# An attention and mixture-of-experts block on one core: expert gates turned on VectorE and fetched back for the biases, and the last batch decoded twice, the second time with weights scaled by ln_g and centred

## Chip, cores and metric

The kernel runs on one core of one Trainium2 chip. The metric is the device time of one execution in microseconds (us), the median of several runs. All arithmetic is float32, but for some bfloat16 copies of bias rows.

## What is computed

Four batches of 512 tokens with 128 channels go through attention and then through a feed-forward part with eight experts, each part with a layer norm before and after and a residual around it:

```python
x = x + ln(attn(ln(x)))                      # one head of 128; ln without weights
x = x + ln(ffn(ln(x)))
# ffn, per token:
spikes = sigmoid(h @ W_enc + b_enc)          # 128 -> 256
cont   = spikes @ W_s2c + b_s2c              # 256 -> 64
probs  = softmax(cont @ Wr + br)             # 8 experts
gate   = top-2 of probs, normalised, 0 for the other six
y      = sum_e gate[e] * (relu(cont @ W1[e] + b1[e]) @ W2[e] + b2[e])
spikes = sigmoid(y @ W_c2s + b_c2s)          # 64 -> 256
decoded = spikes @ W_dec + b_dec             # 256 -> 128
return (decoded - mean) * rsqrt(var + eps) * ln_g + ln_b
```

So the end of a batch has two layer norms in a row: the one of the ffn with `ln_g` and `ln_b` (LN_DEC in the code), and the outer one without weights (LN_Z).

## The kernel before

The program is written engine by engine; each engine runs its list in order and waits on semaphores (`d_` of a DMA, `pe_` of TensorE, `a_` of ScalarE, `v_` of VectorE, `g_` of GpSimd). In the profile TensorE is PE, its weight load PEld, VectorE DVE, ScalarE ACT, GpSimd POOL and SyncE SP. A float32 matmul shows as two MATMUL records. Tokens are in T = 4 tiles of 128; "halves" are tiles 0, 1 and 2, 3. Tiles with a dimension of 2 after the partitions alternate between even and odd batches. The eight PSUM banks are `ps_s` (2), `ps_t`, `ps_a`, `ps_o` (2) and `ps_c` (2).

The batches overlap: while the attention of batch m = b + 2 runs, the experts of batch b are computed, in the loop `for b in range(2)` of each engine's list; after it comes a straight list for the rest of batches 2 and 3.

The gates of a batch take this way. `route` (PE) multiplies into the logits, 8 per token. `router_top`, `router_index` and `router_gates` (DVE, L1175 to L1215) find the two largest and write `gate`, with a token per partition. `turn_gates` (PE, L850) turns the four tiles, so that an expert is a partition. `gate_out` (ACT) copies them to `gateT` (L535), and its DMA (L537, on ACT's queue) writes them to DRAM, eight rows of 2 KB. When that has landed, SP issues five fetches (L379) that broadcast the rows to all 128 partitions of `gate_all`: experts 0, 1, 2 and 3, 4 and 5, 6 and 7, 256 KB an expert. `gate_hidden(b, e)` (DVE, L1224) multiplies the hidden values of expert e in PSUM (from `hidden_pair`, PE, L881) by its gates and writes `gated`, which `expert_out` (PE, L905) takes. `expert_biases` (PE, L899) multiplies `gateT` by `b2_plus` into the same bank first.

The mean over channels of `decoded` is taken out ahead of time: `w_dec` and the bias are centred over the channels, so `decoded` in PSUM has mean zero. Of the last batch, `decode_part` (PE, L934) makes it in halves, `dec_square` (ACT, L561) sums its squares, `dec_var` (DVE, L1245) adds eps, and `inverse_std` (POOL, L406) takes the power -0.5. `dec_scale` (DVE, L1237) multiplies by `ln_g`, `z_scale` (L1254) by the inverse deviation and adds `ln_b`; `z_stats` (L1115 to L1120) takes mean and variance of z, POOL the power again, ACT subtracts the mean (`z_centre`, L574), and `z_add` (L1278) makes the output of that half, which `store` (SP, L371) writes. `x_stats` and `x_norm` (L1127) are the norm at the start of a batch; `turn_x` (PE, L725) waits for it.

## Time and profile before

| | us |
|---|---|
| median of 3 runs (131.42 to 131.71) | 131.65 |
| the profiled execution's own time | 131.94 |
| its span, first to last instruction | 130.1 |
| busy in the span: PE, DVE, ACT, POOL | 118.0, 92.6, 61.3, 30.5 |

The span is what the profile shows; its time is 1.8 us more. Times in rows count from the span's start. "Idle before" in brackets is how long the engine sat idle just before, with what ended it. The profile is of one execution, whose own time is 0.29 us above the median.

### The profile page before, as it was taken

How to read it: one execution, taken by the hardware profiler on the slowest of the kernel's cores; microseconds unless marked ns; L12 is line 12 of the kernel's file. 1: busy time of each engine (PE TensorE's matmuls, PEld its weight loads, DVE VectorE, ACT ScalarE, POOL GpSimd, SP SyncE). 2: the span in 40 equal slices, each digit the busy share in tenths (PEclk: the TensorE clock that was granted, in tenths of full speed). 3: DMA queues.
4: the chain of work that ended last, by engine and by line, in shares of the span. 5: the costliest groups of instructions: out<-in, count | busy, mean ns of one | idle time of the engine just before them, and what ended most of it. 6: DMA issues, size and time to landing. Idle time of an engine off the chain costs nothing.

```text
span 130.1 us, 2478 instructions
## 1 busy us (share of the span) xinstructions
PE 118.0 (91%) x813; PEld 79.4 (61%) x813; DVE 92.6 (71%) x392; ACT 61.3 (47%) x177; POOL 30.5 (23%) x61
## 2 busy tenths in 40 slices
PE   6899999999998999999999998999999999998400
PEld 2556686878645887663677983657566556665300
DVE  0858537698989755888246178968949996689792
...
PEclk9999999999999999999999999999999999999955
...
DMA packets 8843, 12.37 MB, mean 95 GB/s; under 512 B 2641, under 2 KB 5470, under 8 KB 8830
## 3 DMA queue, kind: packets, MB, share of 16 engines
...
q8 instruction: 6, 0.10, 0.3%
...
## 4 chain that ended last, share of the span: by engine, by line
PE 58%; DVE 19%; DMA 8%; POOL 4%; ACT 4%; issue 3%; POOLq 1%; SPq 1%; DVEq 0%
PE ps_t L905 9%; PE ps_s L760 7%; PE ps_o L785 6%; PE ps_s L881 5%; DMA gate_all<-gates 5%; PE ps_o L814 4%; POOL rstd L406 4%; PE ps_t L772 3%; DVE stats L1115 3%; PE ps_c L881 3%; PE ps_c L917 2%; PE ps_a L829 2%; DMA x_in<-in_L_attn_x 2%; DVE gated L1224 2%; ACT probs L495 2%
## 5 line engine op out<-in xcount | busy, mean ns | idle before, releaser
L406 POOL TENSOR_TENSOR rstd<-var_eps,minus_half 128x2 f32<-128x2 f32 (+1 forms) x33 | 25.4, 771 | 93.7 <-DVE var_eps L1120 45.8
L785 PEld LDWEIGHTS ps_o<-v,probsT 128*128 128x128 f32 x128 | 15.7, 191 | 3.5 <-ACT probsT L500 2.5
L785 PE MATMUL ps_o<-v,probsT 128*128 128x128 f32 x128 | 17.5, 279 | 0.1
L905 PE MATMUL ps_t<-gated,w 128*64 128x256 f32 x128 | 16.8, 389 | 0.6 <-DVE gated L1224 0.5
L495 ACT ACTIVATE probs<-ps_s,neg_max 128x512 f32<-128x512 f32 x16 | 11.0, 687 | 11.0 <-DVE neg_max L1143 10.4
L760 PE MATMUL ps_s<-xnT,yT 128*128 128x512 f32 x32 | 16.0, 596 | 0.1
L1143 DVE TENSOR_REDUCE neg_max<-ps_s 128x1 f32<-128x512 f32 x16 | 10.9, 689 | 6.0 <-PE ps_s L760 5.9
L905 PEld LDWEIGHTS ps_t<-gated,w 128*64 128x64 f32 x128 | 8.0, 136 | 8.4 <-DVE gated L1224 4.1
L1224 DVE SCALAR_TENSOR_TENSOR gated<-ps_s,b_minus,gate_all 128x512 f32<-128x512 f32 x14 | 9.9, 745 | 3.3 <-PE ps_s L881 1.8
L516 ACT ACTIVATE spikes<-ps_o,bias_half 128x512 f32<-128x512 f32 x6 | 4.1, 688 | 15.1 <-PE ps_o L814 15.1
L500 ACT ACTIVATE probsT<-ps_t 128x512 f32<-128x512 f32 x16 | 9.5, 592 | 2.0 <-PE ps_t L772 1.8
L772 PE MATMUL ps_t<-ident,probs 128*128 128x128 f32 x64 | 9.8, 276 | 0.2 <-ACT probs L495 0.2
L772 PEld LDWEIGHTS ps_t<-ident,probs 128*128 128x128 f32 x64 | 7.3, 141 | 4.2 <-ACT probs L495 2.4
L1224 DVE SCALAR_TENSOR_TENSOR gated<-ps_c,b_minus,gate_all 128x512 f32<-128x512 f32 x12 | 8.4, 745 | 1.0 <-PE ps_c L881 0.5
L881 PE MATMUL ps_s<-cont,w 64*128 64x256 f32 x56 | 7.9, 401 | 0.0
L541 ACT ACTIVATE moeT<-ps_t 128x256 f32<-128x256 f32 x4 | 1.5, 384 | 12.1 <-PE ps_t L905 12.1
L760 PEld LDWEIGHTS ps_s<-xnT,yT 128*128 128x128 f32 x32 | 5.2, 191 | 2.8 <-issue 2.4
L1155 DVE SCALAR_TENSOR_TENSOR var_eps<-square_sum,eps_term 128x2 f32<-128x2 f32 x8 | 1.3, 164 | 7.4 <-ACT squares L506 7.3
L881 PE MATMUL ps_c<-cont,w 64*128 64x256 f32 x48 | 6.3, 380 | 0.0
L1162 DVE SCALAR_TENSOR_TENSOR x_mid<-ps_o,rstd,x_in 128x128 f32<-128x128 f32 x16 | 4.8, 343 | 2.0 <-POOL rstd L406 2.0
L881 PEld LDWEIGHTS ps_s<-cont,w 64*128 64x128 f32 x56 | 4.8, 186 | 2.1 <-issue 1.5
L1118 DVE BATCH_NORM_AGGREGATE mean_var<-stats 128x2 f32<-128x6 f32 x48 | 6.0, 165 | 0.0
...
## 6 DMA issues: line engine op xcount, KB each, us to landing
gate_all<-gates SPq DMA_DIRECT2D x12, 512.0 KB, 6.2
...
x_in<-in_L_attn_x SPq DMA_DIRECT2D x2, 128.0 KB, 2.7
out<-x_out SPq DMA_DIRECT2D x2, 128.0 KB, 1.8
w_enc<-in_L_ffn_W_enc SPq DMA_DIRECT2D x1, 128.0 KB, 2.8
```

The costliest lines, as they stand in the source:

```text
L406: nc.gpsimd.tensor_tensor(rstd[part], var_eps[part], minus_half[:, t0:t1], ALU.pow).then_inc(g_rstd[n], 1)
L495: nc.scalar.activation(probs[:, b % 2, t], ps_s[:, t % 2], ACT.Exp, bias=neg_max[:, b % 2, t:t + 1], accum_out=prob_sum[:, b % 2, t:t + 1] ...
L500: nc.scalar.activation(probsT[:, b % 2, t], ps_t[:, :].rearrange("p (k q) -> p k q", k=T), ACT.Identity).then_inc(a_pT, 1)
L760: nc.tensor.matmul(ps_s[:, t % 2], yT[:, b % 2, t * P:(t + 1) * P], xnT[:, b % 2], start=True, stop=True).then_inc(pe_s, 1)
L772: mm = nc.tensor.transpose(ps_t[:, k * P:(k + 1) * P], probs[:, b % 2, t, k * P:(k + 1) * P], ident[:, :])
L785: mm = nc.tensor.matmul(attn_out(t), probsT[:, b % 2, t, k], v[:, b % 2, k], start=(k == 0), stop=(k == T - 1))
L814: nc.tensor.matmul(enc_bank(b, c), w_enc[:, c * P:(c + 1) * P], hT[:, b % 2], start=True, stop=True).then_inc(pe_enc, 1)
L881: mm = nc.tensor.matmul(hidden_banks(b, e)[:, h], w1[half, e], cont[half, b % 2], start=True, stop=True)
L905: mm = nc.tensor.matmul(ps_t[h * M:(h + 1) * M, 0:SH], w2[:, e], gated[:, e, h * SH:(h + 1) * SH], start=False, stop=(e == E - 1))
L1118: nc.vector.bn_aggr(mean_var[:, n, b % 2, t], stats[:, n, b % 2, t]).then_inc(v_mv[n], 1)
L1143: nc.vector.tensor_reduce(neg_max[:, b % 2, t:t + 1], ps_s[:, t % 2], AX_X, ALU.max, negate=True).then_inc(v_max, 1)
L1224: nc.vector.scalar_tensor_tensor(token_halves(gated[:, e]), hidden_banks(b, e), b1_minus[:, e:e + 1], token_halves(gate_all[:, b % 2, e]), ...
```

## The change

It has three parts.

*Gates.* `turn_gates` and the copy to `gateT` by ACT are gone for all four batches. DVE writes `gate` with the expert ahead of the tile and turns it in blocks of 32 by 32 into `gate_blocks`, 128 partitions by 32. The DMA on ACT's queue takes that to the same place in DRAM, now as 128 pieces of 128 bytes. SP fetches the eight rows back into `gateT` for `expert_biases`, ahead of the five fetches of `gate_all`.

*Order around the logits of batch 2.* `to_cont(2)` is put between experts 5 and 6 of batch 1, `route(2)` and `hidden_pair(2, 0)` ahead of `to_spikes(1)`. On ACT `cont_out(2)` and `second_exp(2)` go forward, and `cont_out(3)` ahead of `dec_square(1, 0)`. On DVE `z_stats(0, 0)` goes behind the router of batch 2.

*Last batch.* POOL makes `w_dec * ln_g` and `bias * ln_g`, DVE centres these and `ln_b` over the channels (`scaled_weights`), and POOL splits the bias into three bfloat16 rows. After `decode_part` PE decodes both halves again with them. z is then read from PSUM, times the inverse deviation, plus the centred `ln_b`, and has mean zero: `dec_scale`, `z_means` and the subtraction on ACT go away for this batch. The variance of the first half comes from a sum of squares on ACT, of the second from DVE's statistics as before.

```diff
@@ -375,6 +396,10 @@
                 sp.wait_ge(d_gate_out[b], 16)
                 if b >= 2:
                     sp.wait_ge(v_gated, E * (b - 1))
+                    sp.wait_ge(pe_moe, b - 1)
+                else:
+                    sp.wait_ge(g_zero_rows, 4)
+                sp.dma_start(gateT[0:E, b % 2], gates_dram[b].ap()).then_inc(d_gateT[b % 2], 16)
                 for j, (e0, e1) in enumerate(FETCHES):
                     sp.dma_start(gate_all[:, b % 2, e0:e1],
                                  gates_dram[b].ap()[e0:e1].partition_broadcast(P)).then_inc(d_gate_in[b % 2][j], 16)
...
             inverse_std(LN_X, 3, 0)
+            pool.wait_ge(v_wdec, 8)
+            pool.wait_ge(v_bdec, 1)
+            pool.wait_ge(d_ln, 32)
+            nc.gpsimd.tensor_tensor(w_scaled[:, :, :], w_dec[:, :, :],
+                                    g_all[:, :].unsqueeze(1).to_broadcast([P, HC, D]), ALU.mult).then_inc(g_scaled, 1)
+            nc.gpsimd.tensor_tensor(b_scaled[:, :], b_dec_sum[:, :], g_all[:, :], ALU.mult).then_inc(g_scaled, 1)
...
+
+            pool.wait_ge(v_scaled, 2 * (HC + 2) + HC + 2)
+            nc.gpsimd.tensor_copy(b_z_hi[:, :], b_z[:, :]).then_inc(g_bz, 1)
+            pool.wait_ge(g_bz, 1)
+            nc.gpsimd.tensor_tensor(b_z_rest[:, :], b_z[:, :], b_z_hi[:, :], ALU.subtract).then_inc(g_bz, 1)
+            pool.wait_ge(g_bz, 2)
...
             def gate_out(b):
-                act.wait_ge(pe_gT, b + 1)
-                if b == 0:
-                    act.wait_ge(g_zero_rows, 4)
-                if b >= 2:
-                    act.wait_ge(d_gate_out[b - 2], 16)
-                nc.scalar.activation(gateT[0:E, b % 2], gates_bank(b)[0:E], ACT.Identity).then_inc(a_gT, 1)
-                act.wait_ge(a_gT, b + 1)
-                act.dma_start(gates_dram[b].ap(), gateT[0:E, b % 2]).then_inc(d_gate_out[b], 16)
+                act.wait_ge(v_gate_blocks, b + 1)
+                act.dma_start(gates_dram[b].ap().rearrange("e (t j r) -> j (e t) r", t=T, r=32),
+                              gate_blocks[:, b % 2]).then_inc(d_gate_out[b], 16)
...
-            def z_centre(h):
-                act.wait_ge(v_mean, h + 2)
-                for t in range(*HALVES[h]):
-                    nc.scalar.activation(zn[:, (B - 1) % 2, t], z[:, (B - 1) % 2, t], ACT.Identity,
-                                         bias=minus_mean[:, (B - 1) % 2, t:t + 1]).then_inc(a_zn, 1)
+            def z_square():
+                act.wait_ge(v_z, T * (B - 1) + TH)
+                for t in range(TH):
+                    nc.scalar.activation(z_squares[:, t], z[:, (B - 1) % 2, t], ACT.Square,
+                                         accum_out=z_square_sum[:, t:t + 1]).then_inc(a_z_square, 1)
...
@@ -656,16 +698,19 @@
                     exps(m + 1, 1)
                 else:
                     hT_out(3)
-                moe_out(b)
-                cont_out(n)
+                if more:
+                    moe_out(b)
+                    cont_out(n)
+            cont_out(2)
+            moe_out(1)
+            second_exp(2)
             for c in range(HC):
                 spike2(1, c)
-            second_exp(2)
             spike(3, 0)
             spike(3, 1)
             gate_out(2)
+            cont_out(3)
             dec_square(1, 0)
-            cont_out(3)
             dec_square(1, 1)
...
-            def turn_gates(b):
-                pe.wait_ge(v_gate, 9 * (b + 1))
-                if b == 1 or b == 2:
-                    pe.wait_ge(a_c2s, HC * b)
-                for t in range(T):
-                    mm = nc.tensor.transpose(gates_bank(b)[0:E, t * P:(t + 1) * P], gate[:, b % 2, t], ident[:, :])
-                mm.then_inc(pe_gT, 1)
-
...
                 if b < 2:
                     if p == 1:
-                        pe.wait_ge(a_gT, b + 1)
+                        pe.wait_ge(v_logit, b + 1)
+                        pe.wait_ge(a_c2s, HC * b)
...
@@ -884,7 +921,7 @@
 
 
             def expert_biases(b):
-                pe.wait_ge(a_gT, b + 1)
+                pe.wait_ge(d_gateT[b % 2], 16 * (b // 2 + 1))
...
+
+            def decode_scaled(h):
+                b = B - 1
+                t0, t1 = HALVES[h]
+                if h == 0:
+                    pe.wait_ge(g_bz, 7)
+                    pe.wait_ge(v_z1, parts_done(LN_DEC, b - 1, 0))
+                bank = scaled_bank(h)
+                nc.tensor.matmul(bank[:, t0 * P:t1 * P].rearrange("p (t d) -> p t d", d=D), ones_bf[:, :],
+                                 b_z_stack[:, :].unsqueeze(1).to_broadcast([P, t1 - t0, D]), start=True, stop=False)
+                for t in range(t0, t1):
+                    for c in range(HC):
+                        mm = nc.tensor.matmul(bank[:, t * P:(t + 1) * P], spikes2[:, b % 2, c, t * P:(t + 1) * P],
+                                              w_z[:, c], start=False, stop=(c == HC - 1 and t == t1 - 1))
+                mm.then_inc(pe_scaled, 1)
...
-                for e in range(4, E):
-                    expert_out(b, e)
-                to_cont(n)
-                to_spikes(b)
-                route(n)
+                if more:
+                    for e in range(4, E):
+                        expert_out(b, e)
+                    to_cont(n)
+                    to_spikes(b)
+                    route(n)
+            expert_out(1, 4)
+            expert_out(1, 5)
+            to_cont(2)
+            expert_out(1, 6)
+            expert_out(1, 7)
+            route(2)
             hidden_pair(2, 0)
+            to_spikes(1)
             encode(3, 0)
             encode(3, 1)
-            turn_gates(2)
...
@@ -1212,7 +1269,12 @@
                 dve.wait_ge(v_gate, count + 5)
                 nc.vector.tensor_tensor(pick2[:, i], pick2[:, i], wide(w_second), ALU.mult).then_inc(v_gate, 1)
                 dve.wait_ge(v_gate, count + 7)
-                nc.vector.tensor_tensor(gate[:, i], pick1[:, i], pick2[:, i], ALU.add).then_inc(v_gate, 2)
+                nc.vector.tensor_tensor(gate[:, i].rearrange("p e t -> p t e"), pick1[:, i], pick2[:, i],
+                                        ALU.add).then_inc(v_gate, 2)
+                dve.wait_ge(v_gate, count + 9)
+                if b >= 2:
+                    dve.wait_ge(d_gate_out[b - 2], 16)
+                nc.vector.transpose(gate_blocks[:, i], gate[:, i].rearrange("p e t -> p (e t)")).then_inc(v_gate_blocks, 1)
...
+            def scaled_weights():
+                dve.wait_ge(g_scaled, 2)
+                sources = [w_scaled[:, c] for c in range(HC)] + [b_scaled[:, :], b_all[:, :]]
+                results = [w_z[:, c] for c in range(HC)] + [b_z[:, :], b_centred[:, :]]
+                for k, source in enumerate(sources):
+                    nc.vector.bn_stats(scaled_stats[:, k], source).then_inc(v_scaled, 1)
+                dve.wait_ge(v_scaled, HC + 2)
+                for k in range(HC + 2):
+                    nc.vector.bn_aggr(scaled_mean[:, k], scaled_stats[:, k]).then_inc(v_scaled, 1)
+                dve.wait_ge(v_scaled, 2 * (HC + 2))
+                for k, (source, result) in enumerate(zip(sources, results)):
+                    nc.vector.tensor_scalar(result, source, scaled_mean[:, k, 0:1], None, ALU.subtract).then_inc(v_scaled, 1)
+
+            def z_last(h):
+                b = B - 1
+                dve.wait_ge(g_rstd[LN_DEC], parts_done(LN_DEC, b, h))
+                dve.wait_ge(pe_scaled, h + 1)
+                dve.wait_ge(v_scaled, 3 * (HC + 2))
+                for t in range(*HALVES[h]):
+                    nc.vector.scalar_tensor_tensor(z[:, b % 2, t], scaled_bank(h)[:, t * P:(t + 1) * P], inv(LN_DEC, b, t),
+                                                   b_centred[:, :], ALU.mult, ALU.add).then_inc(v_z, 1)
+
+            def z_last_var():
+                dve.wait_ge(a_z_square, TH)
+                nc.vector.tensor_scalar(var_eps[:, LN_Z, (B - 1) % 2, 0:TH], z_square_sum[:, :], 1.0 / D, EPS,
+                                        ALU.mult, ALU.add).then_inc(v_veps[LN_Z], 1)
...
             row_max(3, 0)
             row_max(3, 1)
+            scaled_weights()
             router_top(1)
...
             dec_var(0, 0)
             z_scale(0, 0)
-            z_stats(0, 0)
             router_top(2)
             router_index(2)
             router_gates(2)
+            z_stats(0, 0)
...
             z_add(2, 0)
             dec_var(B - 1, 0)
-            dec_scale(B - 1, 0)
             dec_var(B - 1, 1)
-            z_scale(B - 1, 0)
-            z_stats(B - 1, 0)
-            z_means(B - 1, 0)
-            dec_scale(B - 1, 1)
-            z_scale(B - 1, 1)
+            z_last(0)
+            z_last(1)
+            z_last_var()
             z_stats(B - 1, 1)
-            z_means(B - 1, 1)
             z_add(B - 1, 0)
             z_add(B - 1, 1)
```

Three places of the order. First ACT, from `cont_out(2)` to the gates of batch 3. Here `cont` is written by `cont_out`, `moeT` by `moe_out`, `e` by `second_exp`, `spikes<-ps_c` by `spike2` and `spikes<-ps_o` by `spike`. Before:

```order
L523 ACTIVATE cont<-ps_a,b_cont 128x256
L545 ACTIVATE spikes<-ps_c,bias_half 128x512 x2
L527 ACTIVATE e<-top_diff 128x4
L516 ACTIVATE spikes<-ps_o,bias_half 128x512 x2
L535 ACTIVATE gateT<-ps_c 8x512
L537 DMA gates<-gateT 8x512
L561 ACTIVATE dec_squares,dec_square_sum<-ps_t 128x128 x2
L523 ACTIVATE cont<-ps_a,b_cont 128x256
L561 ACTIVATE dec_squares,dec_square_sum<-ps_c 128x128 x2
L527 ACTIVATE e<-top_diff 128x4
L535 ACTIVATE gateT<-ps_a 8x512
L537 DMA gates<-gateT 8x512
```

Now:

```order
L569 ACTIVATE cont<-ps_a,b_cont 128x256
L583 ACTIVATE moeT<-ps_t 128x256
L573 ACTIVATE e<-top_diff 128x4
L587 ACTIVATE spikes<-ps_c,bias_half 128x512 x2
L562 ACTIVATE spikes<-ps_o,bias_half 128x512 x2
L578 DMA gates<-gate_blocks 4x32x32
L569 ACTIVATE cont<-ps_a,b_cont 128x256
L603 ACTIVATE dec_squares,dec_square_sum<-ps_t 128x128 x2
L603 ACTIVATE dec_squares,dec_square_sum<-ps_c 128x128 x2
L573 ACTIVATE e<-top_diff 128x4
L578 DMA gates<-gate_blocks 4x32x32
```

The copy to `gateT` is gone, and the DMA of batch 2's gates still stands behind both `spikes<-ps_o` of batch 3.

Then PE in the same place: `ps_t<-gated` is `expert_out(1, ...)`, `ps_a<-spikes` is `to_cont`, `ps_c<-moeT` is `to_spikes(1)`, `ps_o<-w_r` is `route(2)`. Before:

```order
L905 MATMUL ps_t<-gated,w 64x256 x8
L829 MATMUL ps_a<-spikes,w_s2c 64x256 x4
L917 MATMUL ps_c<-moeT,w_c2s 128x256 x4
L841 MATMUL ps_o<-w_r,cont 128x8 x4
L881 MATMUL ps_s<-cont,w 128x256 x4
L814 MATMUL ps_o<-hT,w_enc 128x512 x2
L850 MATMUL ps_c<-ident,gate 8x128 x4
L923 MATMUL ps_t<-b_dec_stack,ones_bf 128x256
L950 MATMUL ps_t<-w_dec,spikes 128x128 x4
```

Now:

```order
L942 MATMUL ps_t<-gated,w 64x256 x4
L873 MATMUL ps_a<-spikes,w_s2c 64x256 x4
L942 MATMUL ps_t<-gated,w 64x256 x4
L885 MATMUL ps_o<-w_r,cont 128x8 x4
L918 MATMUL ps_s<-cont,w 128x256 x4
L954 MATMUL ps_c<-moeT,w_c2s 128x256 x4
L858 MATMUL ps_o<-hT,w_enc 128x512 x2
L960 MATMUL ps_t<-b_dec_stack,ones_bf 128x256
L1002 MATMUL ps_t<-w_dec,spikes 128x128 x4
```

The logits of batch 2 come ahead of `to_spikes(1)`; the turn of the gates (`ps_c<-ident,gate`) is gone.

Last DVE at the end of the program, from the first z of the last batch (`dec_var` of both halves stands ahead of it in both, with one `dec_scale` between before). Before:

```order
L1254 SCALAR_TENSOR_TENSOR z<-z,rstd,b_all 128x128 x2
L1115 BN_STATS stats<-z 128x6 x2
L1118 BN_AGGR mean_var<-stats 128x2 x2
L1120 TENSOR_SCALAR var_eps<-mean_var 128x2
L1263 TENSOR_SCALAR minus_mean<-mean_var 128x2
L1237 TENSOR_TENSOR z<-ps_o,g_all 128x256
L1254 SCALAR_TENSOR_TENSOR z<-z,rstd,b_all 128x128 x2
L1115 BN_STATS stats<-z 128x6 x2
L1118 BN_AGGR mean_var<-stats 128x2 x2
L1120 TENSOR_SCALAR var_eps<-mean_var 128x2
L1263 TENSOR_SCALAR minus_mean<-mean_var 128x2
L1278 SCALAR_TENSOR_TENSOR x_out<-zn,rstd,x_mid 128x128 x4
```

Now:

```order
L1343 SCALAR_TENSOR_TENSOR z<-ps_a,rstd,b_centred 128x128 x2
L1343 SCALAR_TENSOR_TENSOR z<-ps_o,rstd,b_centred 128x128 x2
L1348 TENSOR_SCALAR var_eps<-z_square_sum 128x2
L1172 BN_STATS stats<-z 128x6 x2
L1175 BN_AGGR mean_var<-stats 128x2 x2
L1177 TENSOR_SCALAR var_eps<-mean_var 128x2
L1366 SCALAR_TENSOR_TENSOR x_out<-z,rstd,x_mid 128x128 x4
```

With `dec_var` and the first `dec_scale`, the last batch's 20 instructions ahead of its outputs become 12.

## Rows read from the trace of the kernel before

**Rows 1.** The page, parts 1 and 2: busy time, and 40 slices of the span

```profile
PE 118.0 (91%) x813; PEld 79.4 (61%) x813; DVE 92.6 (71%) x392; ACT 61.3 (47%) x177; POOL 30.5 (23%) x61
...
PEclk9999999999999999999999999999999999999955
```

**Rows 2.** Chain of waits, 60 to 82 us: start, us, what

```profile
70.28 0.45 PE ps_c L850 x4
...
71.37 1.45 DMA gates<-gateT
...
73.67 5.95 DMA gate_all<-gates
...
79.72 0.76 DVE gated L1224
```

**Rows 3.** Timeline, 36 to 60 us: start, us, engine line op out<-in xcount

```profile
44.62 1.01 POOL L406 TENSOR_TENSOR rstd<-var_eps,minus_half 128x4 f32<-128x4 f32 x1 [5.55 <-DVE var_eps L1120]
...
46.09 1.10 DVE L1127 TENSOR_SCALAR xn<-x_in,mean_var,rstd 128x128 f32<-128x128 f32 x4
```

**Rows 4.** Timeline, 0 to 36 us

```profile
12.57 0.54 POOL L426 TENSOR_SCALAR w_s2c<-w_s2c_raw 128x128 f32<-128x128 f32 x1
12.62 0.60 DVE L1127 TENSOR_SCALAR xn<-x_in,mean_var,rstd 128x128 f32<-128x128 f32 x2 [0.33 <-POOL rstd L406]
```

**Rows 5.** Timeline, 60 to 82 us

```profile
66.16 0.19 DVE L1175 TENSOR_TENSOR logits<-ps_o,br_all 128x32 f32<-128x32 f32 x1 [3.47 <-PE ps_o L841]
...
69.92 0.60 ACT L500 ACTIVATE probsT<-ps_t 128x512 f32<-128x512 f32 x1
...
70.11 0.60 PE L850 MATMUL ps_c<-ident,gate 128*8 128x128 f32 x4
...
70.56 1.16 PE L785 MATMUL ps_o<-v,probsT 128*128 128x128 f32 x8
...
80.52 1.31 PE L905 MATMUL ps_t<-gated,w 128*64 128x256 f32 x8 [0.55 <-DVE gated L1224]
```

**Rows 6.** Timeline, 82 to 105 us

```profile
93.18 0.69 ACT L516 ACTIVATE spikes<-ps_o,bias_half 128x512 f32<-128x512 f32 x1 [0.17 <-PE ps_o L814]
...
94.36 0.27 ACTq L537 DMA_DIRECT2D gates<-gateT  x1
...
100.01 1.41 DVE L1224 SCALAR_TENSOR_TENSOR gated<-ps_s,b_minus,gate_all 128x512 f32<-128x512 f32 x2
...
101.47 1.41 DVE L1224 SCALAR_TENSOR_TENSOR gated<-ps_c,b_minus,gate_all 128x512 f32<-128x512 f32 x2
```

**Rows 7.** Timeline of SP's queue, 95 to 98 us

```profile
95.82 2.22 SPq L379 DMA_DIRECT2D gate_all<-gates  x5
```

**Rows 8.** DMA issues of 96.6 to 97.05 us: size, us to landing

```profile
gate_all<-gates SPq DMA_DIRECT2D x1, 512.0 KB, 4.7
```

**Rows 9.** DMA issues of the whole span: size, us to landing

```profile
out<-x_out SPq DMA_DIRECT2D x2, 128.0 KB, 1.8
...
b_qk<-in_L_attn_bk ACTq DMA_DIRECT2D x1, 0.5 KB, 3.1
```

**Rows 10.** Timeline, 120.6 us to the end

```profile
120.66 1.06 PE L934 MATMUL ps_o<-w_dec,spikes 128*128 128x128 f32 x8
...
120.86 1.14 DVE L1278 SCALAR_TENSOR_TENSOR x_out<-zn,rstd,x_mid 128x128 f32<-128x128 f32 x4 [0.34 <-POOL rstd L406]
...
122.16 1.36 POOL L406 TENSOR_TENSOR rstd<-var_eps,minus_half 128x2 f32<-128x2 f32 x2 [1.33 <-DVE var_eps L1245]
...
122.89 0.61 DVE L1254 SCALAR_TENSOR_TENSOR z<-z,rstd,b_all 128x128 f32<-128x128 f32 x2 [0.30 <-POOL rstd L406]
123.53 0.49 DVE L1115 BATCH_NORM_STATS2 stats<-z 128x6 f32<-128x128 f32 x2
...
126.57 0.80 POOL L406 TENSOR_TENSOR rstd<-var_eps,minus_half 128x2 f32<-128x2 f32 x1 [1.35 <-DVE var_eps L1120]
...
127.40 0.61 DVE L1278 SCALAR_TENSOR_TENSOR x_out<-zn,rstd,x_mid 128x128 f32<-128x128 f32 x2 [0.26 <-POOL rstd L406]
```

More of the change, by code:

```diff
@@ L229, in c2s_done, with scaled_bank @@
             return b + 1 + (c if b == B - 1 else 0)
+        def scaled_bank(h):
+            return ps_o[:, 1] if h else ps_a
         d_x = [[sem(f"d_x{b}{i}") for i in range(1 if b else 2)] for b in range(B)]
@@ L243, in attention_moe_block @@
         d_ln = sem("d_ln")
+        d_gateT = [sem(f"d_gateT{i}") for i in range(2)]
         d_gate_out = [sem(f"d_gate_out{b}") for b in range(B)]
@@ L257, in attention_moe_block @@
         g_out = sem("g_out")
+        g_scaled = sem("g_scaled")
+        g_bz = sem("g_bz")
         pe_wqk = sem("pe_wqk")
@@ L682, in _ @@
                 dec_square(B - 1, h)
-            for h in range(2):
-                z_centre(h)
+            z_square()
         @block.tensor
@@ L1031, in _ @@
                     turn_h(n)
-                if more:
-                    turn_gates(b)
                 scores(m, 3)
-                if not more:
-                    turn_gates(b)
                 attend(m, 1)
@@ L1107, in _, with statistics @@
                 decode_part(3, h)
+            for h in range(2):
+                decode_scaled(h)
         @block.vector
         def _(dve):
-            def statistics(n, b, i, source):
+            def statistics(n, b, i, source, elsewhere=0):
                 t0, t1 = parts(n, b)[i]
```

46 lines of the change are left out of this document (33 added, 13 removed).

## The prediction

> **What bounds the kernel now.** I read the page first: PE is busy 118.0 of 130.1 us at full clock until the last two slices, where the granted clock is 0.5 (1.2 in place of 2.4 GHz) and PE has no work left [rows 1]. So what shortens the kernel is PE work taken out where PE is not waiting for something else, and the tail behind PE's last matmul. Then the chain of waits shows where that is so. Around the gates of batch 1 it leaves PE: the turn of the gates ends at 70.73, the write to DRAM goes out at 71.37 and lands 1.45 later, and the third fetch of `gate_all` lands at 79.62, just before `gate_hidden(1, 2)` at 79.72 [rows 2]. The timeline shows PE idle 0.55 behind it [rows 5]. In batch 2 the fetch of experts 2 and 3, the first of 512 KB, is issued at about 96.7 and takes 4.7 [rows 7, 8]: it lands at about 101.4, and its reader starts at 101.47 [rows 6]. The fetches are thus nearly the limit in both. In the tail, from PE's last matmul (ends 121.72) to the last output (127.40 + 0.61 = 128.01), one chain goes DVE, POOL, DVE, POOL, DVE [rows 10].
>
> I count against the profiled execution: 131.94 us, 0.29 above the median of 131.65. A difference of 0.2% is about what a measurement of this kernel can tell from no change.
>
> **Gates of batch 0: gain 0.2.** Four turns go, 0.45 of PE's time by the group of batch 1 in the chain [rows 2]. PE comes that much earlier to `turn_x(3)`, which waits for `x_norm(3)`. That starts at 46.09 and could not before POOL's power ends at 45.63 [rows 3], and this power moves later by the new turn on DVE, which stands ahead of it. The trace has no such instruction. The nearest is DVE's sum on 128x32, 0.19 [rows 5]; I take 0.2. Its ends are 0.1 (most of the 0.19 hidden under its neighbours) and 0.3 (a pass over 128x128, 0.61 for two [rows 10]). So `x_norm(3)` starts at about 45.87: gain 0.22, between 0.1 and 0.45. The fetches of batch 0 are not waited for.
>
> **Gates of batch 1: gain 0.3.** The turns at 70.11 go, but `attend(3, 1)` behind them, at 70.56, needs `probsT`, which ACT ends at 70.52 [rows 5]: PE gains 0.15, not 0.45. The rest depends on the fetches. The write goes out at 70.55, right behind `probsT`, in place of 71.37: 0.8 earlier, as ACT's copy and PE's turn are out of its way. It now has 128 pieces of 128 bytes. Bounds for issue to landing: 1.45, the write of today [rows 2], and 3.1, 128 single floats at the start, beside many other loads [rows 9]. A store of 128 rows to DRAM takes 1.8 with eight times the bytes [rows 9]; the write is nearest to that, and I take 1.7. Then SP issues the fetch of `gateT` first: an issue costs 0.44 (five in 2.22 [rows 7]) for 128 rows, I take 0.3 for eight. Sum: 0.8 - 0.25 - 0.3 = 0.25 earlier, and `gate_hidden(1, 2)` starts 0.3 before 79.72. PE would be there 0.15 earlier and waits all the longer. Ends: a loss of 1.1 with a landing of 3.1, a gain of 0.7 if the fetches keep up (0.15 and the 0.55 of idle time).
>
> The Trainium skill (DMA: Bandwidth & Descriptors, Specifications) asks for 512 bytes or more for line rate and says that below it the DMA does a read-modify-write. It gives no time for a write as small as this, and no row here is of one. By that rule the write goes towards its upper end, which is the second rival with its 133.05; by the store's row the sum stands as below.
>
> **Gates and logits of batch 2: gain 0.1.** The logits come about 1.0 earlier, since `to_spikes(1)` stands behind them, not ahead. But the write stands on ACT behind both `spikes` of batch 3, the last of which ends at 93.87 [rows 6]; the new order keeps PE's sum of work ahead of them. So the write goes out at about 93.95 in place of 94.36, 0.4 earlier, and lands 0.15 earlier after a longer flight; with the issue of `gateT` the fetches start 0.15 **later**. PE and DVE behind are about 0.3 earlier (0.5 of turns less 0.2 of DVE's turn for batch 3, which stands between the router and `gate_hidden(2, 0)` at 100.01 [rows 6]). The fetch of experts 2 and 3 takes this back: its reader starts at about 101.6, not 101.47, and PE, which computes a hidden pair ahead of the experts that need it and so has some slack, keeps 0.1. Ends: -0.2 and +0.45; with a landing of 3.1, -1.4. The earlier logits pay nothing by themselves.
>
> **Gates of batch 3: 0.** PE's turns stood while it waited for `gate_hidden(2, 0)`. `expert_biases(3)` comes long after its fetch.
>
> **Prepared weights: 0.** POOL makes two products after the power that ends at 45.63 [rows 3], three times the elements of the 0.54 at 12.57 [rows 4], so some 1.5 us; POOL is busy 23% of the span [rows 1], and rival 4 has the case where they hurt. DVE's four statistics and four subtractions on 128x128, 1.0 and 1.2 us by the 0.49 and the 0.61 for two [rows 10], and four small ones between stand ahead of the router of batch 1, where DVE is idle 3.47 [rows 5]. That cover of about 1 us is gone if PE's logits come over 0.8 earlier. POOL's seven on the bias rows lie far from any power that is waited for.
>
> **The tail: gain 0.9.** Before: z of half 0 at 122.89 [rows 10], the end at 128.01, 5.12 later. Now:
> - PE decodes again from 121.72, 1.06 a half by the row at 120.66 plus 0.1 of bias (an estimate: the records of the bias and the first matmul overlap): ends 122.85 and 123.95, still at full clock, as the fall comes only in the slices from 123.6 on, with PE idle since 121.72 [rows 1, 10].
> - z of half 0 is still bound by POOL's power (122.16 + 0.7): 122.89 to 123.50, at 0.61 as before.
> - z of half 1 waits for PE: 123.97 to 124.58. ACT's two squares lie beside it.
> - variance of half 0 0.1, then statistics of half 1: 0.92, as from 123.53 to the power behind them in the old order. Ends 125.62.
> - POOL's power of half 1: 125.70, 0.80 [rows 10], to 126.50; half 0's output 125.65 to 126.26.
> - half 1's output 126.53 to 127.14.
>
> 128.01 - 127.14 = 0.87. If PE were not the limit of z of half 1 it would be 1.3; if the second decoding takes 0.3 longer, 0.6.
>
> **Sum:** 0.22 + 0.30 + 0.10 + 0.87 = 1.49. 131.94 - 1.49 = 130.45, and against the median 131.65 - 1.49 = 130.16: I say 130.2. Its own range is 129.6 to 131.0.
>
> **Rivals.**
> 1. *All of PE's time comes back* (DVE's turn is short, the write lands in 1.45 or less, fetches never bind): 0.45 + 0.70 + 0.45 + 1.3 = 2.9, 128.75. For it: fetches have their start 0.8 earlier. Against: the margin of batch 2 is 0.1. Chance 0.14.
> 2. *The write of 128 small pieces lands late* and takes the place of PE's turns. Each us of it costs up to two, once in batch 1 and once in batch 2, as both wait for their fetches now. The gain of 1.49 is gone at 0.7 to 0.75 more than my 1.7, at a landing of 2.4 to 2.5. At 3.1: +0.22 - 1.1 - 1.4 + 0.87 = -1.4, 133.05. For it: 128 rows of 4 bytes took 3.1. Against: that was in the crowd of the first loads. Chance 0.09.
> 3. *Only the tail and little else*: fetches half a us later than I have them, a gain of 0.6 to 0.9 in all, 131.0. Chance 0.12.
> 4. *POOL's new work holds up DVE.* `w_scaled` runs just when DVE does `x_norm(3)`, for which PE waits. At its price of about 0.9 (128x256, from 0.54 for half as much) the gain falls to 0.6 or, with a second collision in batch 2, to 0.3: 131.3. Against: `x_norm` took the same 0.60 for two beside POOL's `w_s2c` at 12.57 [rows 4] as it takes for half of its 1.10 for four at 46.09 [rows 3]. Chance 0.05. The Trainium skill (SBUF — State Buffer, Who interferes with whom) has it that GpSimd and VectorE share one pair of ports and that whoever comes second blocks for the whole instruction, if VectorE's is in a two-port mode or has two inputs in SBUF; by that rule this rival would be likelier than the rows make it.
>
> **Chances.** Forecast 0.60, rivals 0.14, 0.09, 0.12, 0.05. Faster by over 0.2% (below 131.39): forecast, 1, 3 and part of 4, 0.87; within: 0.04; slower: rival 2, 0.09. The range reaches to rival 1's middle and takes in 3 and 4: 129.0 to 131.5.
>
> **What would show it.** The gates' write: issue to landing 1.6 to 1.8 in batch 1, and `gate_hidden(1, 2)` still waiting for its fetch with PE idle some 0.7. DVE waiting for the fetch ahead of `gate_hidden(2, 2)`. The last matmul about 2.2 behind the end of `decode_part`, at full clock; z of half 1 released by PE, not POOL; 0.9 less from z of half 0 to the end. I am wrong if PE's stretch ahead of `decode_part` ends more than 1.5 earlier (rival 1) or later than before (rival 2).

## The result and the profile after

The changed kernel takes 130.78 us (median of 6 runs, 130.59 to 132.68), the kernel before, run beside it, 131.82 (131.42 to 132.07): a ratio of 0.9917, 95% interval 0.9891 to 0.9943. That is faster by 1.1 us. (The ratio leaves out runs that lie over 1.5% above the fastest of their kernel, here the one of 132.68.) The profiled execution has 130.91 of its own and a span of 129.0, against 131.94 and 130.1.

The page's busy times and PE's clock, of the changed kernel (before: [rows 1]):

```profile
PE 118.7 (92%) x815; PEld 80.1 (62%) x815; DVE 94.4 (73%) x400; ACT 58.8 (46%) x173; POOL 33.8 (26%) x70
...
PEclk9999999999999999999999999999999999999998
```

PE has 0.7 us more to do, the second decoding less the turns of the gates, and the kernel is still shorter. The timeline of the changed kernel, first from the logits of batch 0 to the experts of batch 0:

```profile
38.17 0.19 DVE L1232 TENSOR_TENSOR logits<-ps_c,br_all 128x32 f32<-128x32 f32 x1
...
44.82 1.01 POOL L431 TENSOR_TENSOR rstd<-var_eps,minus_half 128x4 f32<-128x4 f32 x1 [5.79 <-DVE var_eps L1177]
...
45.80 0.73 POOL L469 TENSOR_TENSOR w_scaled<-w_dec,g_all 128x256 f32<-128x256 f32 x1
...
45.87 1.67 DVE L1184 TENSOR_SCALAR xn<-x_in,mean_var,rstd 128x128 f32<-128x128 f32 x4 [0.17 <-POOL rstd L431]
...
46.49 0.46 POOL L471 TENSOR_TENSOR b_scaled<-b_dec_sum,g_all 128x128 f32<-128x128 f32 x1
...
54.34 2.21 PE L942 MATMUL ps_t<-gated,w 128*64 128x256 f32 x16
```

`x_norm(3)` starts 0.22 earlier, as forecast (0.19 counted from the logits), and then takes 1.67 in place of 1.10 [rows 3]: it runs beside POOL's two products. Next, the gates of batch 1 and their fetches (ACTq and SPq are the issues of DMAs):

```profile
70.06 0.60 ACT L546 ACTIVATE probsT<-ps_t 128x512 f32<-128x512 f32 x1
...
70.38 0.53 ACTq L578 DMA_DIRECT2D gates<-gate_blocks  x1
...
72.33 0.29 SPq L402 DMA_DIRECT2D gateT<-gates  x1
...
72.66 2.22 SPq L404 DMA_DIRECT2D gate_all<-gates  x5
...
79.31 1.40 DVE L1286 SCALAR_TENSOR_TENSOR gated<-ps_c,b_minus,gate_all 128x512 f32<-128x512 f32 x2
```

The write takes 0.53 to issue, and the fetch of `gateT` follows 1.95 behind the write's start. `gate_hidden(1, 2)`, at 79.31, shows no idle time before it: DVE comes to it straight from its other work, and the fetch that it needs, issued at 73.49, has landed after 5.5 us, at 79.0. PE's rows alone show `expert_out(1, 0)` to `(1, 3)` in one piece. In `after_again`, the same kernel once more (experiment 1), DVE waits 0.30 for that fetch and PE 0.40 for DVE; before it was 0.45 and 0.55. The row of PE in `after`, then DVE's and PE's in `after_again`:

```profile
78.93 2.49 PE L942 MATMUL ps_t<-gated,w 128*64 128x256 f32 x16
```

```profile
79.79 1.41 DVE L1286 SCALAR_TENSOR_TENSOR gated<-ps_c,b_minus,gate_all 128x512 f32<-128x512 f32 x2 [0.30 <-DMA gate_all<-gates]
80.59 1.31 PE L942 MATMUL ps_t<-gated,w 128*64 128x256 f32 x8 [0.40 <-DVE gated L1286]
```

Then the output of batch 0 and the router of batch 3:

```profile
94.66 0.29 POOL L480 CAST b_z_hi<-b_z 128x128 bf16<-128x128 f32 x1
...
94.74 1.49 DVE L1366 SCALAR_TENSOR_TENSOR x_out<-zn,rstd,x_mid 128x128 f32<-128x128 f32 x4 [0.35 <-POOL rstd L431]
...
95.04 0.43 POOL L482 TENSOR_TENSOR b_z_rest<-b_z,b_z_hi 128x128 f32<-128x128 f32 x1
...
95.81 0.52 PEld L885 LDWEIGHTS ps_o<-w_r,cont 64*128 64x128 f32 x8
...
96.82 0.17 DVE L1232 TENSOR_TENSOR logits<-ps_o,br_all 128x32 f32<-128x32 f32 x1
...
99.68 1.38 DVE L1286 SCALAR_TENSOR_TENSOR gated<-ps_s,b_minus,gate_all 128x512 f32<-128x512 f32 x2
...
100.46 1.31 PE L942 MATMUL ps_t<-gated,w 128*64 128x256 f32 x8 [0.84 <-DVE gated L1286]
...
100.98 1.40 DVE L1286 SCALAR_TENSOR_TENSOR gated<-ps_c,b_minus,gate_all 128x512 f32<-128x512 f32 x2
```

In batch 2 PE now waits 0.84 for DVE's first `gated`, and DVE comes to `gate_hidden(2, 2)`, at 100.98, without idle time, so without a wait for the fetch.

And the tail (before: [rows 10]):

```profile
122.31 1.06 PE L986 MATMUL ps_o<-w_z,spikes 128*128 128x128 f32 x8
122.54 0.61 DVE L1343 SCALAR_TENSOR_TENSOR z<-ps_a,rstd,b_centred 128x128 f32<-128x128 f32 x2 [0.31 <-POOL rstd L431]
...
123.81 0.61 DVE L1343 SCALAR_TENSOR_TENSOR z<-ps_o,rstd,b_centred 128x128 f32<-128x128 f32 x2 [0.66 <-POOL rstd L431]
...
125.31 0.61 DVE L1366 SCALAR_TENSOR_TENSOR x_out<-z,rstd,x_mid 128x128 f32<-128x128 f32 x2
125.44 0.77 POOL L431 TENSOR_TENSOR rstd<-var_eps,minus_half 128x2 f32<-128x2 f32 x1 [0.17 <-DVE var_eps L1177]
126.25 0.61 DVE L1366 SCALAR_TENSOR_TENSOR x_out<-z,rstd,x_mid 128x128 f32<-128x128 f32 x2 [0.33 <-POOL rstd L431]
```

**Where executions agree, and where not.** Two things differ by chance from execution to execution. In the thirteen profiles of this study DVE's `logits` of batch 0 start at 37.95 to 38.52 us (two of them at 39.90 and 39.98); from there to `expert_out(0, 0)` each version repeats within 0.02. And the length from the issue of batch 1's `gate_all` fetches to `gate_hidden(1, 2)`, called the flight below, is 6.34 to 7.17, with no order among the versions. It is set by the fetches only where DVE waits for them. In three profiles (`after`, `pool_moved_again`, `tail_pool_moved`) DVE does not, and there `gate_hidden(1, 2)` stands 24.97 to 24.99 behind `expert_out(0, 0)`. Before it stands 25.52 behind, so 0.55 is the most that fetches can give at this place. So I read lengths between marks, not times from the span's start. The two marks of before, to set beside 38.17 and 54.34:

```profile
38.20 0.19 DVE L1175 TENSOR_TENSOR logits<-ps_c,br_all 128x32 f32<-128x32 f32 x1
...
54.20 2.21 PE L905 MATMUL ps_t<-gated,w 128*64 128x256 f32 x16
```

| Stretch, us | before | after | after_again | shift | forecast |
|---|---|---|---|---|---|
| logits of batch 0 to `expert_out(0, 0)` | 16.00 | 16.17 | 16.17 | +0.17 | -0.22 |
| to the issue of batch 1's `gate_all` | 18.64 | 18.32 | 18.31 | -0.32 | -0.25 |
| flight, to `gate_hidden(1, 2)` | 6.89 | 6.65 | 7.03 | chance | 0 |
| to the end of `decode_part` | 42.00 | 42.05 | 42.06 | +0.05 | -0.15 |
| to z of half 0 | 1.17 | 1.18 | 1.18 | 0.01 | 0 |
| to the end of the last output | 5.13 | 4.32 | 4.32 | -0.81 | -0.87 |

Without the flight the whole is 0.88 shorter (the shifts, rounded one by one, add up to 0.90); with it, 1.11 and 0.73 (89.81 in all before, 88.70 and 89.08 after). (The forecast put 0.3 and 0.1 on batches 1 and 2, whose parts here are 0.25 of the fetches' start, and 0.15 behind it.)

### The profile page after: what moved, and what is told of

It is laid out like the page before. It is cut to its first block, busy times and chain, and to the rows that moved or that the text cites. A ratio compares the mean times of both kernels' runs of the same rounds, so it can differ in the third digit from the quotient of the medians.

```text
span 129.0 us, 2501 instructions
## 1 busy us (share of the span) xinstructions
PE 118.7 (92%) x815; PEld 80.1 (62%) x815; DVE 94.4 (73%) x400; ACT 58.8 (46%) x173; POOL 33.8 (26%) x70
## 3 DMA queue, kind: packets, MB, share of 16 engines
HBM read 11.16 MB, written 1.11 MB: 95 GB/s over the span
## 4 chain that ended last, share of the span: by engine, by line
PE 54%; DVE 23%; issue 8%; POOL 7%; ACT 3%; DMA 2%; POOLq 1%; DVEq 0%
PE ps_t L942 10%; POOL rstd L431 7%; PE ps_s L804 6%; PE ps_o L829 6%; PE ps_s L918 5%; PE ps_c L918 4%; DVE stats L1172 3%; PE ps_o L858 3%; PE ps_t L816 3%; DVE x_out L1366 2%; DMA x_in<-in_L_attn_x 2%; DVE xn L1184 2%; PE ps_o L918 2%; PE ps_a L769 2%; DVE neg_max L1200 2%
## 5 line engine op out<-in xcount | busy, mean ns | idle before, releaser
L1184 DVE TENSOR_SCALAR xn<-x_in,mean_var,rstd 128x128 f32<-128x128 f32 x16 | 5.2, 375 | 1.2 <-POOL rstd L431 0.9
```

The source lines that it names most:

```text
L1184: nc.vector.tensor_scalar(result(t), source(t), mean_var[:, n, b % 2, t, 0:1], inv(n, b, t), ALU.subtract, ALU.mult).then_inc(done, 1)
```

## Experiments

Each ran in five rounds beside the kernel before. Times of marks are lengths from DVE's logits of batch 0, or between marks, as above.

**1. The change once more.** No edit.

> The changed kernel once more, as the measure for the others on this chip. Both theories: 0.9917 of the kernel before, within 0.003.

Median 131.05, ratio 0.9923 (0.9894 to 0.9951). The result repeats. The profile is the column of the table: every length is that of the first but the flight, 0.38 longer. A gain or a loss of 0.4 in one profile at that place says nothing.

**2. The tail alone.** The gates and the order as before.

```diff
-                act.wait_ge(v_gate_blocks, b + 1)
+                act.wait_ge(pe_gT, b + 1)
+                nc.scalar.activation(gateT[0:E, b % 2], gates_bank(b)[0:E], ACT.Identity).then_inc(a_gT, 1)
...
+            def turn_gates(b):
...
                 nc.vector.tensor_tensor(gate[:, i], pick1[:, i], pick2[:, i], ALU.add).then_inc(v_gate, 2)
-                nc.vector.transpose(gate_blocks[:, i], gate[:, i].rearrange("p e t -> p (e t)")).then_inc(v_gate_blocks, 1)
```

> The kernel before with the last batch's part alone (prepared weights, second decoding). Theory A (the tail gives 0.8 us, and GpSimd's two products beside x_norm(3) take back 0.4 to 0.6, since VectorE waits for them): 0.2 to 0.5 us faster than before, ratio 0.996 to 0.9985, and x_norm(3) takes about 1.65 us for its four in place of 1.10. Rival B (GpSimd's products cost nothing, the delay near x_norm(3) in the changed kernel is from the gates' part): 0.8 us faster, ratio 0.994, x_norm(3) 1.10.

Median 131.9, ratio 0.9988 (0.9949 to 1.0026): no difference, so neither expectation had the time (0.2 to 0.5 or 0.8 faster), and `x_norm(3)` took 1.25, not 1.65 or 1.10. From z of half 0 to the end it has 3.97, which is 1.16 less than before. All of that is lost ahead of it: the profile's end of `decode_part` is 1.17 later. Of this 0.32 is a later start of the whole (logits of batch 0 at 38.52), 0.29 the flight (7.17), and 0.55 lies in batch 2, from `expert_out(1, 2)` to the end of `decode_part` (41.75 in place of 41.20). There POOL's operations on `b_z` fall beside the router of batch 2:

```profile
92.49 0.29 POOL L483 CAST b_z_mid<-b_z_rest 128x128 bf16<-128x128 f32 x1
92.52 0.42 DVE L1269 TENSOR_SCALAR e_sum<-e 128x4 f32<-128x4 f32 x1
...
93.39 0.27 DVE L1276 TENSOR_TENSOR pick<-pick,w_second 128x32 f32<-128x32 f32 x1
93.70 0.42 POOL L490 TENSOR_TENSOR b_z_stack<-b_z_rest,b_z_mid 1x128 bf16<-1x128 f32 x1
93.76 0.40 DVE L1278 TENSOR_TENSOR gate<-pick 128x32 f32<-128x32 f32 x1
```

The same three of DVE's operations in experiment 5, which has the old order too, with POOL quiet:

```profile
91.12 0.16 DVE L1271 TENSOR_SCALAR e_sum<-e 128x4 f32<-128x4 f32 x1
...
91.72 0.19 DVE L1278 TENSOR_TENSOR pick<-pick,w_second 128x32 f32<-128x32 f32 x1
92.02 0.19 DVE L1280 TENSOR_TENSOR gate<-pick 128x32 f32<-128x32 f32 x1
```

0.42, 0.27 and 0.40 in place of 0.16, 0.19 and 0.19: 0.55 in all. `x_norm(3)` lost only 0.14 here, since it starts at 46.40, after most of the first product, and `expert_out(0, 0)` comes as before (16.00).

**3. The gates alone.** Order and tail as before.

```diff
-            expert_out(1, 4)
-            expert_out(1, 5)
-            to_cont(2)
-            expert_out(1, 6)
-            expert_out(1, 7)
-            route(2)
...
-            for h in range(2):
-                decode_scaled(h)
...
-            scaled_weights()
```

> The kernel before with the gates' part alone (turned on VectorE, written in 128 pieces, biases' rows fetched ahead), the order of work as before and the last batch as before. Theory A (the gates' part is worth 0.8 to 1.1 us by itself: 0.2 at batch 0, 0.5 at the fetch of batch 1, 0.2 to 0.4 in batch 2): ratio 0.991 to 0.994. Rival B (without the moved logits the gates' part gains little, as the fetches of batch 2 start later): 0.5 us or less, ratio 0.996 or more.

Median 131.51, ratio 0.9978 (0.9942 to 1.0014), unclear by itself. The lengths are not: `expert_out(0, 0)` comes 15.62 behind the logits, 0.37 earlier than before, and batch 1's `gate_all` is issued another 0.31 earlier. Batch 2 is 0.15 longer (41.35): PE waits 0.38 ahead of `route(3)` for ACT's `cont` (experiment 6 has the same wait). By the lengths the part is worth 0.37 + 0.31 - 0.15 = 0.53, without what the flight does: B's "0.5 us or less", not the 0.8 to 1.1 of A, though A's 0.2 at batch 0 was too low. The timeline of this kernel, `x_norm(3)` without products beside it:

```profile
44.82 1.01 POOL L431 TENSOR_TENSOR rstd<-var_eps,minus_half 128x4 f32<-128x4 f32 x1 [5.79 <-DVE var_eps L1145]
...
45.86 1.12 DVE L1152 TENSOR_SCALAR xn<-x_in,mean_var,rstd 128x128 f32<-128x128 f32 x4 [0.17 <-POOL rstd L431]
...
53.79 2.21 PE L920 MATMUL ps_t<-gated,w 128*64 128x256 f32 x16
```

**4. POOL's new work elsewhere.** The products and the operations on `b_z` stand between POOL's powers for batches 2 and 3, where DVE does nothing that PE waits for. `products_moved` moves the two products alone.

```diff
             inverse_std(LN_X, 3, 0)
+            for h in range(2):
+                inverse_std(LN_ATT, 2, h)
+                inverse_std(LN_MID, 2, h)
             pool.wait_ge(v_wdec, 8)
...
             nc.gpsimd.tensor_tensor(b_scaled[:, :], b_dec_sum[:, :], g_all[:, :], ALU.mult).then_inc(g_scaled, 1)
-            for m in (2, 3):
-                for h in range(2):
-                    inverse_std(LN_ATT, m, h)
-                    inverse_std(LN_MID, m, h)
...
             pool.wait_ge(g_bz, 7)
+            for h in range(2):
+                inverse_std(LN_ATT, 3, h)
+                inverse_std(LN_MID, 3, h)
```

> The changed kernel with GpSimd's two products and its seven bias operations put between its powers of batches 2 and 3, where VectorE has little to do. Theory A (they block VectorE beside x_norm(3) and beside the output of batch 0): 0.4 to 0.7 us faster than the changed kernel, ratio to before 0.986 to 0.989; x_norm(3) back at 1.10 for four, the output of batch 0 at 1.14. Rival B (TensorE was bound by something else there): same time as the changed kernel, 0.991 to 0.992, though x_norm(3) is at 1.10.

> The changed kernel with only POOL's two products (w_scaled, b_scaled) moved from before the powers of batch 2 to between those of batches 2 and 3; the seven operations on b_z stay where the change has them, beside DVE's output of batch 0. Theory A (two-input operations of POOL hold up DVE wherever the two meet, and it costs time where PE waits for DVE): both places count. Here only the first is mended: the four subtractions of x_norm(3) take 1.10 again, expert_out(0, 0) starts 0.2 to 0.3 earlier than in the kernel before (0.14 later in the changed kernel), but z_add(0, 0) still takes some 1.45 and DVE's logits of batch 3 stay 0.4 to 0.5 behind PE's; the time lies between the changed kernel and pool_moved, about 0.2 us from each. Theory B (only x_norm(3) matters): as pool_moved, 1.5 us faster than the kernel before in its profile.

`pool_moved`: median 130.45, ratio 0.9876 (0.984 to 0.9912); once more on another chip (`pool_moved_again`), 130.49, 0.9916 (0.9875 to 0.9958). `products_moved`: 130.55, 0.9939 (0.9899 to 0.998). These intervals overlap, and the lengths tell them apart. (Against the changed kernel the time tells too: on their common chip ten of the runs of `pool_moved` are 129.97 to 131.06, eleven of `after_again` 130.86 to 131.38.) To `expert_out(0, 0)`: 15.61, 15.62 and 15.62, against 16.17 in the changed kernel, so the products cost 0.55. From `expert_out(1, 2)` to the end of `decode_part`: 41.04 and 40.93 with all of it moved, 41.26 with the products alone moved, as in the changed kernel: the operations on `b_z` cost another 0.27. Both places count, theory A (its gain at `expert_out(0, 0)`, 0.2 to 0.3 on the kernel before, was 0.37). `pool_moved`, the same operations as shown of the changed kernel:

```profile
44.96 1.01 POOL L431 TENSOR_TENSOR rstd<-var_eps,minus_half 128x4 f32<-128x4 f32 x1 [5.78 <-DVE var_eps L1179]
...
46.00 1.11 DVE L1186 TENSOR_SCALAR xn<-x_in,mean_var,rstd 128x128 f32<-128x128 f32 x4 [0.16 <-POOL rstd L431]
```

```profile
94.58 1.14 DVE L1368 SCALAR_TENSOR_TENSOR x_out<-zn,rstd,x_mid 128x128 f32<-128x128 f32 x4 [0.35 <-POOL rstd L431]
...
95.66 0.61 PE L887 MATMUL ps_o<-w_r,cont 64*128 64x8 f32 x8
...
96.32 0.19 DVE L1234 TENSOR_TENSOR logits<-ps_o,br_all 128x32 f32<-128x32 f32 x1
```

`x_norm(3)` has its 1.11 again, the output of batch 0 1.14 (1.49 beside POOL), and DVE takes the logits of batch 3 as PE ends them.

**5. The tail alone, with POOL's work moved.** Experiment 2 with the edit of 4.

> tail_only (the new tail alone, gates and order as in the kernel before) with POOL's products and its seven operations on b_z moved to between the powers of batches 2 and 3, as in pool_moved. Theory A (what tail_only lost ahead of its tail, 1.17 us to the end of decode_part, came from POOL's two-input operations beside DVE): the end of decode_part lies within 0.3 of the kernel before, and the time is 0.9 to 1.2 us below it. Theory B (it came from elsewhere: DVE's new work on the weights, or how the fetches happened to land): the end of decode_part is still 0.6 or more later, and the time within 0.6 of the kernel before.

Median 131.09, ratio 0.9948 (0.9917 to 0.998); profile 130.31 of its own. `expert_out(0, 0)` at 16.00, batch 2 at 41.19, the tail 3.97. The end of `decode_part` came 0.79 earlier than before, 0.25 by an early start and 0.55 by the shortest flight of all, 6.34 (DVE waits for no fetch there), so the "0.3" of theory A has to be read without these: it is 0.00. Theory A's time was missed: the ratio is worth 0.7 us, with an interval of 0.3 to 1.1, below its 0.9 to 1.2; by the lengths it should be 1.16. Theory B falls by the lengths: the weights' other work on DVE costs nothing, and the 0.55 of experiment 2's batch 2 was POOL.

**6. The order.** `pool_moved` with the order of before, and once more on the chip of `pool_moved_again`. ACT's part and PE's:

```diff
             gate_out(2)
+            dec_square(1, 0)
             cont_out(3)
-            dec_square(1, 0)
...
-            expert_out(1, 4)
-            expert_out(1, 5)
-            to_cont(2)
-            expert_out(1, 6)
-            expert_out(1, 7)
-            route(2)
             hidden_pair(2, 0)
-            to_spikes(1)
             encode(3, 0)
```

> pool_moved with the order of the work as in the kernel before (the logits of batch 2 behind to_spikes(1), moe_out and second_exp back), the new way of the gates and the new tail kept. Theory A (the early logits are worth the earlier write of batch 2's gates): the write goes out 0.4 later, gate_hidden(2, 2) 0.3 to 0.4 later, the end of decode_part 0.2 to 0.3 later than in pool_moved. Theory B (they pay nothing, the prediction's reading): within 0.1 of pool_moved at the end of decode_part. Theory C (with the early logits DVE comes late to other work): the old order is faster by 0.1 or more.

> pool_moved_old_order once more. Theory A (the early logits are worth something): from the write of batch 1's gates to the end of decode_part 0.1 to 0.3 longer than in pool_moved_again. Theory B (nothing): within 0.1.

Medians 130.46 and 130.63, ratios 0.9928 (0.9877 to 0.998) and 0.9923 (0.9879 to 0.9968), against 130.49 for `pool_moved_again` beside the second: 0.14, nothing that the times can tell. `expert_out(1, 2)` to the end of `decode_part`: 41.19 and 41.28, against 41.04 and 40.93. (From the write of batch 1's gates, as asked of the second, it is 51.43 against 50.65, but 0.42 of this is the flight.) So the order is worth about 0.25, theory A's size, but in the changed kernel the operations on `b_z` took it back. Theory A's reason is not what the traces show. The write of batch 2's gates goes out 12.78 behind `expert_out(1, 2)`, against 12.70: 0.1 later, not 0.4. What is 0.26 later are DVE's logits of batch 3 (16.63 against 16.37), and ahead of them PE waits for ACT, whose `cont_out(3)` stands behind `dec_square(1, 0)` in this order. PE's row in `pool_moved_old_order`, then ACT's:

```profile
95.53 0.61 PE L884 MATMUL ps_o<-w_r,cont 64*128 64x8 f32 x8 [0.22 <-ACT cont L571]
```

```profile
94.48 0.28 ACT L605 ACTIVATE dec_squares<-ps_t 128x128 f32<-128x128 f32 x1 [1.57 <-DVE z L1290]
...
95.00 0.47 ACT L571 ACTIVATE cont<-ps_a,b_cont 128x256 f32<-128x256 f32 x1
```

In `pool_moved` the same row of PE, at 95.66 (experiment 4), has no wait. So the gain lies where ACT's `cont_out(3)` was put forward. No run moves that alone, and none shows a gain from the early logits of batch 2 themselves.

**7. The output of batch 0 later.** `pool_moved` with 2 us of DVE's work moved from ahead of the logits of batch 3 to batch 3's gates.

```diff
-            z_centre(0)
-            z_add(0, 0)
             dec_scale(1, 0)
...
                 gate_hidden(3, e)
+                if e == 3:
+                    z_centre(0)
+                    z_add(0, 0)
```

> pool_moved with z_centre(0) and z_add(0, 0), 2.0 us of DVE, moved from before dec_scale(1, 0) to behind the fourth gate_hidden of batch 3. Theory A (with POOL's operations gone from beside it, DVE reaches the logits of batch 3 as PE gives them): DVE's logits stay at PE's end, gate_hidden(2, 0) and the end of decode_part stay within 0.1 of pool_moved, the time is the same. Theory B (DVE's queue is what holds the router of batch 3, and POOL's operations only made it worse): gate_hidden(2, 0) 0.3 or more earlier than in pool_moved, the time 0.3 shorter.

Median 130.53, ratio 0.9906 (0.9871 to 0.9941). `expert_out(1, 2)` to the end of `decode_part` 40.94: as `pool_moved` (41.04 and 40.93), theory A. With POOL out of the way DVE's queue has the room, and what cost time was that POOL stretched it. (In this profile and the next the logits of batch 0 come 1.6 to 1.7 us later than in `pool_moved`; the lengths behind them are not touched.)

**8. The fetches later.** `pool_moved` with one more fetch of the gates' rows, waited for ahead of `gate_all`.

```diff
                 sp.dma_start(gateT[0:E, b % 2], gates_dram[b].ap()).then_inc(d_gateT[b % 2], 16)
+                sp.dma_start(gate_again[0:E], gates_dram[b].ap()).then_inc(d_again, 16)
+                sp.wait_ge(d_again, 16 * (b + 1))
```

> pool_moved with a second fetch of the eight gate rows that is waited for ahead of the gate_all fetches of every batch: they start some 2.0 us later. Theory A (the fetches of batches 1 and 2 bind both times with hardly any slack, as the prediction's price of up to two us for one of landing has it): gate_hidden(1, 2) 1.9 to 2.0 later than in pool_moved, another 1.5 to 1.9 at the experts of batch 2, 3.4 to 3.9 us in all. Theory B (the first delay moves everything behind it, so the second finds slack, or PE's own work covers much): 2.0 to 2.5 us in all.

Median 134.78, ratio 1.0208 (1.0154 to 1.0262). SP's queue in this kernel, then in `pool_moved`:

```profile
73.52 0.29 SPq L404 DMA_DIRECT2D gateT<-gates  x1
73.85 0.30 SPq L405 DMA_DIRECT2D gate_again<-gates  x1
75.45 2.91 SPq L408 DMA_DIRECT2D gate_all<-gates  x5
```

```profile
71.91 0.29 SPq L402 DMA_DIRECT2D gateT<-gates  x1
72.24 2.22 SPq L404 DMA_DIRECT2D gate_all<-gates  x5
```

In `fetch_later` the `gate_all` fetches go 1.93 behind that of `gateT`, in `pool_moved` 0.33: 1.60 later, not 2.0 (in batch 2 1.89 against 0.33, 1.56 later). `expert_out(1, 2)` comes 43.07 behind the logits against 41.64 and 41.39 in the two of `pool_moved`, 1.4 to 1.7 later; the rest to the end of `decode_part` is 42.91, 1.9 longer. Of this 1.9, 1.6 to 1.7 has come by the first expert of batch 3, and 0.25 lies behind it, where the fetches of batch 3 are late too. So 1.6 twice cost 3.3 to 3.7: theory A, both times nearly all of it and a little more. The prediction's price for a late write, up to two us for one, holds.

## Why the prediction was right or wrong

The chance of faster, the range and the side were right: 130.78 lies in 129.0 to 131.5, 0.6 above the 130.2, and inside the forecast's own 129.6 to 131.0. That the number came so near has luck in it. By the lengths the kernel is 0.88 shorter, not 1.49: 0.82 was lost to a cost that the sum had at 0, and gains larger than forecast (batch 0, the order) made up part of it. The flight gave another 0.2 in one profile and took 0.1 in the other. The steps:

- **Gates of batch 0, gain 0.2: the step is worth 0.37, and POOL took 0.55.** The turn on DVE takes 0.21, as taken from the 0.19 [rows 5], and `x_norm(3)` started 0.2 earlier. But that PE comes to wait for it was not so before: `tail_only` ended `x_norm(3)` 0.14 later and lost nothing at `expert_out(0, 0)`. PE therefore kept 0.37 of its 0.45 (`gates_only`), nearly my upper end.
- **Prepared weights 0: this is the step that failed.** The products cost 0.55 at `x_norm(3)`, the `b_z` operations 0.27 in batch 2. I had them as 1.5 us beside a DVE that is not disturbed, by `x_norm` beside `w_s2c` [rows 4], and wrote that the seven on the bias rows lie far from any power that is waited for. That asks who waits for POOL, and leaves out whom POOL holds up. The row could not stand for them: `w_s2c` is a TENSOR_SCALAR of one tile, the products are TENSOR_TENSOR of two, though no run tells that this is the difference that counts. Rival 4, at 0.05, had the mechanism and both places; its price of 0.9 was too high for the first (0.55; POOL took 0.73 and 0.46), and the two places together cost 0.82. The Trainium skill (SBUF — State Buffer, Who interferes with whom) says that DVE with two inputs in SBUF, beside a POOL instruction that reads SBUF, or DVE in a two-port mode, and POOL exclude one another for a whole instruction. That agrees with `x_out` in the sum (two inputs, 1.49 for 1.14), but its first tile, begun 0.08 behind POOL's cast of 94.66, took 0.36, about the 0.35 that it takes without POOL. `x_norm(3)` has one input, so by the rule it must be in a two-port mode, which no run here shows. Even so the rule deserved more than 0.05.
- **Gates of batch 1, gain 0.3: the start of the fetches was right, both of its terms off, and PE's own share was nothing.** From logits of batch 1 to the write's issue 4.08, in place of 5.21: 1.13 earlier, not 0.8, as the queue of ACT issues the write while `probsT` still runs (70.38, beside 70.06 to 70.66). From the write to the first `gate_all` 2.28, in place of 1.46: 0.82 longer, not 0.55. The write lands after 1.9, I had 1.7, between 1.45 and 3.1. Net 0.31 against 0.25. The 0.15 of PE did not come: `attend(3, 1)` starts 16.36 behind `expert_out(0, 0)` before and 16.37 now, and before it already stood 0.04 behind the end of `probsT` (70.56 and 70.52 [rows 5]), so by my own rows the turns hardly held it up. Counted from `expert_out(0, 0)`, `gate_hidden(1, 2)` came 0.55 earlier in one profile, all there is to gain, and 0.17 in the next. The sign "still waiting for its fetch with PE idle some 0.7" did not come in the first, and in the second PE waited 0.40. Rival 2 is out: 1.9 is short of its 2.4. The Trainium skill's (DMA: Bandwidth & Descriptors, Specifications) read-modify-write below 512 bytes would show as this longer write; what part of the 0.5 it is, no run here tells, since the old write had 8 pieces and this has 128.
- **Batch 2, gain 0.1: came out as nothing,** 41.26 in place of 41.20. The parts are larger than the sum: the order gives 0.25, `b_z` takes 0.27, and the gates' new way, in the old order, takes 0 to 0.15 (41.35 in `gates_only`, 41.19 and 41.28 in experiment 6). The working was off too. Counted from `expert_out(1, 2)`, the write goes out 1.14 earlier, not 0.4 (12.70 for 13.84: here too ACT's queue issues it while the last `spikes` runs, 92.80 beside 92.05 to 93.49), and the fetches start 0.34 **earlier** (14.96 for 15.30), not 0.15 later. The sign "DVE waiting for the fetch ahead of `gate_hidden(2, 2)`" did not come. PE waits for DVE at `gate_hidden(2, 0)` instead (0.84), and POOL's work beside the output of batch 0 has made DVE later there. "The earlier logits pay nothing by themselves" stands undecided: the 0.25 shows where ACT's `cont_out(3)` went forward.
- **The tail, gain 0.87: 0.81.** The second decoding runs at full clock and ends 2.0 behind `decode_part` (123.37), 0.2 sooner than forecast, and z of half 0 is bound by POOL. z of half 1 I had 1.08 behind that of half 0; it is 1.27. In the two kernels without the new gates it is 0.92, and the tail 3.97. PE ends 0.83 behind the start of z of half 0 with and without the new gates, and with them 0.35 more pass before DVE starts (POOL's power of half 1 ends at 123.18, PE at 123.37, DVE starts at 123.81). I did not find the cause; without it the tail would have given 1.16.
- Rival 1, with 2.9, is out: even with POOL's work moved the kernel gains 1.1 to 1.6. Rival 3 gave 131.0 and is near the time by chance: the gates and the order did give 0.37, 0.31 and 0.25, and POOL's 0.82 took most of it.

With POOL's work moved the sum is 0.37 + 0.31 + 0.25 - 0.1 + 0.81 = 1.64, and `pool_moved` measures 0.9876 and 0.9916, 1.6 and 1.1 us below the kernel before. On their common chip its median is 0.60 below `after_again` (130.45 and 131.05).
